# A cross-attention kernel's scores: from one f32 product to three f16 products, with another order of steps

## The reference

```python
# x: (64, 32, 256); ctx_1024: (64, 257, 128); H = 16 heads of D = 128
h = layernorm(x)
q = rmsnorm((h @ Wq).reshape(B, 32, 16, 128), gq)
k = rmsnorm((ctx @ Wk).reshape(B, 257, 16, 128), gk)
v = (ctx @ Wv).reshape(B, 257, 16, 128)
scores = einsum("bqhd,bkhd->bhqk", q, k) / sqrt(128)
x = x + (softmax(scores) @ v).reshape(B, 32, 2048) @ Wo
x = x + self_attention(layernorm(x))        # ternary weights, rope, causal, 32 tokens
x = x + moe(layernorm(x))                   # 8 experts, capacity 256, and a shared one
```

## Time and profile before

| | |
|---|---|
| runs, median (lowest to highest) | 1541.29 us (1538.57 to 1545.86) |
| profiled execution, its own time | 1538.1 us |
| its span | 1536.3 us |
| mean granted TensorE clock | 0.936 |
| TensorE busy | 1295.5 us, 84% |
| VectorE busy | 1005.7 us, 65% |
| ScalarE busy | 841.6 us, 55% |
| GpSimd busy | 538.5 us, 35% |

### The profile page before, as it was taken

One profiled execution on the slowest core, in us unless ns is written; L12 is line 12 of the kernel. 1 busy time (PEld: TensorE's weight loads), 2 busy tenths in 40 slices (PEclk: granted clock), 3 DMA queues, 4 the chain that ended last, 5 costly groups with the idle time before them and its releaser, 6 DMA issues.

```text
span 1536.3 us, 35628 instructions
## 1 busy us (share of the span) xinstructions
PE 1295.5 (84%) x10526; PEld 881.2 (57%) x10526; DVE 1005.7 (65%) x3748; ACT 841.6 (55%) x3560; POOL 538.5 (35%) x1337
## 2 busy tenths in 40 slices
PE   5768898989899898989898989888898989864881
PEld 2545666566666556565666565656565565643761
DVE  6846677677767677777777776777776767743112
ACT  5365566656475656666565666475656556631110
POOL 2044342524352534435243525342524325310003
PEclk9998999999999999999999999999999989985996
DMA  9000000000010101000001000000101000100544
GB/s 372 22 26 12 23 15 25 17 25 17 11 32 10 32 7 30 13 25 17 21 14 28 14 25 18 14 28 11 31 7 35 7 25 14 62 6 23 168 146 127
DMA packets 41191, 59.65 MB, mean 39 GB/s; under 512 B 5094, under 2 KB 35953, under 8 KB 40096
## 3 DMA queue, kind: packets, MB, share of 16 engines
q1 hardware_dynamic: 36880, 50.73, 10.3%
q0 software_dynamic: 2064, 6.14, 1.2%
q10 hardware_dynamic: 2176, 2.10, 0.4%
HBM read 48.62 MB, written 10.49 MB: 38 GB/s over the span
## 4 chain that ended last, share of the span: by engine, by line
PE 33%; issue 25%; POOL 16%; DVE 9%; ACT 5%; DMA 3%; POOLq 1%; SPq 0%; DVEq 0%; ACTq 0%
PE AB L594 21%; PE Eb L594 5%; POOL prob L1177 4%; PE Db L594 4%; ACT prob L1020 2%; DMA ctxn<-expert_rows 2%; POOL pjunk L1132 2%; PE C L719 1%; POOL cn_lo L1197 1%; DVE o_halves L1492 1%; POOL rstd L1152 1%; ACT rkb L1014 1%; POOL cl_rows L1212 1%; POOL c_lo L1138 1%; DVE kst L1312 1%
## 5 line engine op out<-in xcount | busy, mean ns | idle before, releaser
L950 ACT ACTIVATE AB<-AB 128x128 f32<-128x128 f32 (+1 forms) x1160 | 303.7, 262 | 185.4 <-PE AB L594 182.9
L1132 POOL TENSOR_TENSOR pjunk<-pjunk 128x1 f32<-128x1 f32 x288 | 56.3, 196 | 683.9 <-DVE sinv L1482 365.9
L594 PE MATMUL AB<-wk_hi,c_hi 128*128 128x512 f16 x512 | 199.7, 390 | 22.0 <-POOL c_lo L1138 8.8
L1312 DVE BATCH_NORM_STATS2 kst<-AB 128x6 f32<-128x256 f32 x512 | 181.3, 415 | 55.4 <-PE AB L594 50.9
L950 ACT ACTIVATION_READ_ACCUMULATOR AB<-AB 128x1 f32 (+1 forms) x1160 | 216.0, 186 | 0.0
L594 PE MATMUL AB<-wk_lo,c_hi 128*128 128x512 f16 x512 | 198.5, 388 | 0.0
L594 PE MATMUL AB<-wk_hi,c_lo 128*128 128x512 f16 x512 | 197.5, 386 | 0.0
L594 PE MATMUL AB<-ctxT,qpT 128*128 128x257 f32 x512 | 161.6, 472 | 35.5 <-DVE sc L1547 27.4
L1020 ACT ACTIVATE prob<-prob,nbias,rq 128x257 f32<-128x257 f32 x256 | 150.4, 590 | 7.9 <-DVE nbias L1477 7.9
L594 PEld LDWEIGHTS AB<-ctxT,qpT 128*128 128x128 f32 x512 | 115.2, 236 | 60.6 <-DVE sc L1547 29.1
L1177 POOL TENSOR_SCALAR prob<-prob,sinv 128x257 f32<-128x257 f32 x256 | 128.7, 503 | 20.2
(11 more groups left out here) (252 smaller groups left out, 2933.9 us busy)
## 6 DMA issues: line engine op xcount, KB each, us to landing
ctxT<-in_ctxT SPq DMA_DIRECT2D x64, 128.5 KB, 2.1
ctxn<-in_ctxn SPq DMA_DIRECT2D x64, 128.0 KB, 2.1
wq_hi<-in_w SPq DMA_DIRECT2D x4, 768.0 KB, 5.3
wq_lo<-in_w SPq DMA_DIRECT2D x4, 768.0 KB, 5.6
expert_rows<-base POOLq DMA_DIRECT2D x1, 2048.0 KB, 15.8
xin<-in_x SPq DMA_DIRECT2D x16, 128.0 KB, 2.2
prob<-in_wqT SPq DMA_DIRECT2D x1, 2048.0 KB, 19.2
xres<-in_x SPq DMA_DIRECT2D x16, 128.0 KB, 2.0
```

What stands on the lines that cost most here:

```text
L594: return pe.matmul(out, lhsT, rhs, start=start, stop=stop)
L950: ins = nc.scalar.activation(k, k, ACT.Square, accum_out=sums[0:m, h:h + 1])
L1132: own.mark(pool.tensor_tensor(pjunk[:, 0:1], pjunk[:, 1:2], pjunk[:, 1:2], ALU.mult))
L1312: ins = V.bn_stats(stats[:, 0, 2 * half + n], AB[0:m, 2 + half, 2 * D * n:2 * D * (n + 1)])
```

## The change

The projected queries are kept as two f16 halves instead of one f32 value. ScalarE's copy in QP now writes the high half and leaves the bank filled; VectorE has a new step QP, which subtracts the high half from the bank, writes the low half and gives the bank back. A score bank is now made by three f16 matmuls, high by high, high by low and low by high, from the halves `c_hi` and `c_lo` of the keys that GpSimd has made already. And all four lists of the loop are in another order; in the first fill only VectorE's new QP is put in.

```diff
@@ ORDER, the list of VectorE, before and after @@
-    "DVE": """K0 X K1 K2 dp3 XL K3 KN0 Q do3 RQ f K4 K5 qkv K6 s0 i0 sc s1 sm K7 KN1 ys yv i1 dp0 pr ln2 do0 dp1
-              s2 lg do1 i2 up pos s3 dn dp2 do2 i3""".split(),
+    "DVE": """K0 X K1 K2 XL dp3 K3 do3 KN0 Q RQ f K4 K5 K6 qkv QP s0 K7 KN1 i0 sc s1 sm dp0 ys yv s2 pr ln2 i1 s3
+              i2 do0 up lg dp1 dn pos i3 do1 dp2 do2""".split(),
...
-        qpT = sb("qpT", [P, NB, H * SQ])
+        qpT = sb("qpT", [P, 2, NB, H * SQ], F16)
...
+        qp_ready = Events(sem("qp_ready"), pro=BANKS, full=BANKS)
...
+        def query_part(e, n):
+            return qpT[:, e, :, 4 * SQ * n:4 * SQ * (n + 1)].rearrange("p b (h q) -> p h b q", q=SQ)
+
+        def by_query(n):
+            return AB[:, n].rearrange("p (h b q) -> p h b q", b=NB, q=SQ)
...
-                    mm(AB[:, g, 0:SKV], qpT[:, b, P * g:P * (g + 1)], ctxT[:, SKV * b:SKV * (b + 1)])\
-                        .then_inc(filled[s].sem, 1)
+                    q_hi, q_lo = (qpT[:, e, b, P * g:P * (g + 1)] for e in range(2))
+                    keys_hi, keys_lo = (c[:, SKV * b:SKV * (b + 1)] for c in (c_hi, c_lo))
+                    mm(AB[:, g, 0:SKV], q_hi, keys_hi, stop=False)
+                    mm(AB[:, g, 0:SKV], q_hi, keys_lo, start=False, stop=False)
+                    mm(AB[:, g, 0:SKV], q_lo, keys_hi, start=False).then_inc(filled[s].sem, 1)
...
-                    nc.scalar.copy(dst, src).then_inc(drained[s].sem, 1)
+                    nc.scalar.copy(query_part(0, n), by_query(n)).then_inc(qp_ready.sem, 1)
...
+            def step_QP(p):
+
+                for n, s in enumerate(BANKS):
+                    dve.wait_ge(qp_ready.sem, qp_ready.at(p, s))
+                    V.tensor_tensor(query_part(1, n), by_query(n), query_part(0, n), ALU.subtract).then_inc(drained[s].sem, 1)
```

More of the change, by code:

```diff
@@ L149 @@
 ORDER = {
[L150 to L153, removed]
-    "DVE": """K0 X K1 K2 dp3 XL K3 KN0 Q do3 RQ f K4 K5 qkv K6 s0 i0 sc s1 sm K7 KN1 ys yv i1 dp0 pr ln2 do0 dp1
-              s2 lg do1 i2 up pos s3 dn dp2 do2 i3""".split(),
-    "POOL": """h1 h0 c2 n3 h2 X c3 r0 cl ln1 c0 h3 r1 n0 c1 r2 y n1 ln2 r3 n2 scat""".split(),
+    "PE": """K0 pt3 K1 K2 X K3 o3 Q f K4 K5 xt1 K6 qkv rk1 rk0 QP qk s0 K7 sc s1 rk2 pt0 pv s2 st pr rk3 s3 o0
+              xt2 up lg pt1 dn pos o1 pt2 o2""".split(),
+    "ACT": """K0 tl3 K1 K2 X ph3 K3 oh3 Q K4 K5 xt1 K6 qkv rk1 rk0 QP qk K7 e0 sc rk2 ph0 tl0 pv e1 rk3 e2 xt2 oh0
+              up ph1 tl1 lg e3 oh1 ph2 tl2 oh2""".split(),
+    "DVE": """K0 X K1 K2 XL dp3 K3 do3 KN0 Q RQ f K4 K5 K6 qkv QP s0 K7 KN1 i0 sc s1 sm dp0 ys yv s2 pr ln2 i1 s3
+              i2 do0 up lg dp1 dn pos i3 do1 dp2 do2""".split(),
+    "POOL": """h0 n3 h1 X h2 c1 c3 c0 r1 ln1 h3 c2 r0 cl r2 n0 r3 y ln2 n1 n2 scat""".split(),
 }
@@ L164 @@
               K7 ph1 tl1 oh0 rk2 e2 rk3 oh1 e3 ph2 tl2 oh2""".split(),
-    "DVE": """low wk KL KNL K0 K1 X K2 XL wql K3 gg KN0 Q W0l wt0 W1l K4 RQ wt1 M01 wt K5 M23 tw s0 s1 i0 K6 dp0
+    "DVE": """low wk KL KNL K0 K1 X K2 XL wql K3 gg KN0 Q W0l wt0 W1l K4 QP RQ wt1 M01 wt K5 M23 tw s0 s1 i0 K6 dp0
               i1 K7 KN1 do0 dp1 s2 s3 i2 dp2 do1 i3 do2""".split(),
@@ L445, in build @@
         fin = [x[:, :].rearrange("p b n -> p (b n)").rearrange("p (a c) -> p a c", c=DIM) for x in
-               (qpT, rkx[:].rearrange("p a k n -> p (a k) n"))]
+               (qpT[:].rearrange("p e b n -> p e (b n)").bitcast(F32), rkx[:].rearrange("p a k n -> p (a k) n"))]
         fin = [f[:, 4 * k:4 * k + 4] for f in fin for k in range(2)]
@@ L956, in step_QP @@
                     act.wait_ge(filled[s].sem, filled[s].at(p, "QP"))
-                    dst = qpT[:, :, 4 * SQ * n:4 * SQ * (n + 1)].rearrange("p b (h q) -> p h b q", q=SQ)
-                    src = AB[:, n].rearrange("p (h b q) -> p h b q", b=NB, q=SQ)
-                    nc.scalar.copy(dst, src).then_inc(drained[s].sem, 1)
+                    nc.scalar.copy(query_part(0, n), by_query(n)).then_inc(qp_ready.sem, 1)
             def step_X(p):
@@ L1629, in step_dn @@
                 V.tensor_tensor(base[:], x2[:], Eb[:, 0:DIM], ALU.add).then_inc(drained["E"].sem, 1)
-            steps = dict(X=step_X, XL=step_XL, Q=lambda p: key_stats(p, "Q", P, qst), RQ=step_RQ,
+            steps = dict(X=step_X, XL=step_XL, Q=lambda p: key_stats(p, "Q", P, qst), RQ=step_RQ, QP=step_QP,
                          wql=step_wql, W0l=lambda p: step_Wl(p, 0), W1l=lambda p: step_Wl(p, 1), f=step_f, qkv=step_qkv, sc=step_sc, sm=step_sm, ys=step_ys, yv=step_yv,
```

## The result

The changed kernel took 1525.3 us, the median of 7 runs (1523.58 to 1530.19), beside 1541.3 us for the kernel before: a ratio of 0.991, 95% interval 0.988 to 0.994. One of the seven runs of the kernel before that were timed beside it, 1620.6 us, stands far above the other six (1534.5 to 1545.9) and is not in the ratio.

The account below looks back on a forecast made before the run. It took the loop as half bound by TensorE, half by a chain through VectorE. 1538.1 less 15 for the loop plus 2 for the ends gave 1525, in the median about 1528; it said 1527, range 1501 to 1552.

Parts of the forecast that it names:

- 1.0 a tile: Loop: a tile of 81.1 us against 82.0 to 82.2, taken as 15 us over fifteen tiles.
- The score products: TensorE's score steps: 1.73 to 1.30 us each at full clock, 1.7 us a tile, up to 2.6.
- Nothing hides it: VectorE's four subtractions between qkv and s0: 0.62 us each, 2.5 a tile, covered only by what TensorE does meanwhile.
- Rival (3): Subtraction on VectorE at its upper bound, 1.03 us each: 1.6 us more a tile, 1551 us; chance 0.10.
- The walk: One tile followed in the new order: K0 to QP 37.7 us, pv at 59.4, then 21.7 to the next K0.
- "+1" for the first fill: First fill: four subtractions (2.5 us) behind VectorE's K4, TensorE's score steps 1.7 shorter; 1 us longer.
- "+1" for the last tile: Last tile: up and dn come ahead of pos, so the experts' scatter is about 1 us later.
- s2, if it stays at half clock, 0.8: Between pv and the next K0: s2's shorter score products take 0.8 us off if the half clock remains.
- Rival (2): Half clock lasting until pr and o0: about 1.7 us a tile, 25 above the forecast, 1552 us; chance 0.09.
- the rule of the Trainium skill: TensorE's clock: throttled by default, released by activity; shorter score products and longer waits around sc speak against the change.

Follow-up runs that it names:

- the kernel with the fill's edit alone: Changed kernel with VectorE's QP moved behind RQ in the first fill only; 1521.6 us, 0.988 of the kernel before.
- the kernel of two products with extra matmuls: Changed kernel without the low-by-high score product, plus 13 unread matmuls a tile behind sc and rk2; 1524.3 us, 0.991 of the kernel before.

## Why the prediction was right, and where its terms were wrong

The number, 1527 against 1525.3, is as near as it is by luck: its errors offset each other. The loop gives 23.9 us in 14 periods where 1.0 a tile was taken (14), and the last tile 1.9 where nothing was left (1.0 less 1); against that the fill costs 7.0 where 1 was, and the experts' part 5.0 where none was.

**The score products** were right: 1.32 us a step at full clock, 0.33 a bank, 2.55 at half. Between the f32 and the f16 kernel in the new order they give 1.6 us a tile of the 1.7 that they hold.

**"Nothing hides it"** was wrong as the new order has it. The size of the subtraction was right, 0.62 us. But "VectorE's chain gets 2.5 us longer while TensorE's work gets 1.7 us shorter" sets against each other two things that lie side by side. QP and qk end on TensorE at the same time whether VectorE subtracts meanwhile or not: s0 starts 43.3 us behind K0 in the f32 kernel in the new order and 43.4 in the changed one. The sentence holds in the old order, where K6 waits 2.04 us and a tile gains nothing. The walk itself had both paths, K7 on TensorE and the statistics at 49.0 (48.4 measured), so the sum did not suffer from it. Rival (3) was not far off in its price for all that: with 0.2 us of cover left at s0's last bank, 0.41 more for each of four would have put about 1.4 us on the path (an estimate from these two numbers).

**The walk**, K0 to QP 37.7, to pv 21.7, to K0 21.7, measured 37.1, 21.9 and 21.6 in the tile shown. The 0.6 is in the first stretch, in waits that came out 0.9 shorter together, with 0.3 of small gaps against them that were not followed: pt3 was to wait 0.5 for n3 and waits under 0.2 (K0's twelve products end at 774.93 + 2.6 = 777.5, pt3 starts at 777.69), so n3 does not hold it up, rk0 0.4 and waits 0.24, K5 1.71 and waits 1.23. From QP to pv the waits came out singly too: 1.07, 2.16, 0.53 us before sc, before s1 and before pt0 (0.5 to 1.5 there over the 14 tiles), where 1.0, 2.4 and 0.9 were said. The other 0.1 of the 0.7 by which the gain of a tile was short is the base: "82.0 to 82.2" is the steady tile, as the median is, and the loop's mean before is 82.3 by its one period of 85.6.

**"+1" for the first fill** is the term that was most mis-sized. It counted four subtractions of 0.62 as work. They stand in line behind QP's banks, so the step lasts from the first to the last bank, 5.2 us with what it waits, and RQ and the weight work behind it come as much later. A row that tells of it stood in the trace before: ScalarE's copy of a bank waits 0.86 us for TensorE.

**"+1" for the last tile** was wrong in its sum. With the loop's last turn in it, which the sum counted as its fifteenth tile, that part should have come out even, and took 1.9 us less. The turn itself lasts the same in both traces (80.5 and 80.6 us from K0 to the end of o2). Behind it, pr to the last scatter takes 17.3 us where it took 15.7, later as the term says (16.5 in the kernel with the fill's edit alone), but o2 to pr takes 39.4 instead of 43.0, which the term left out: pt3 there waits 1.3 us for GpSimd instead of 5.1, since i3 and with it n3 come earlier in the new lists (n3 itself waited 4.3 us for i3 before, and after not at all). Giving the router its old order back is worth 0.3 to 0.4.

**The clock.** "s2, if it stays at half clock, 0.8" was left open; it got its full clock back, and with the order alone. From pv to pr it takes 4.6 us before and 3.5 in the new order with either product, but hardly for the clock: in three tiles of the kernel before s2 has its full clock already, and these take 4.35. The rest fits KN1, which stood on VectorE between sm and ys (754.94 to 758.09) and is now ahead of sc. Rival (2), the half clock that lasts into pr, costs what was said, about 1.7 us a tile (medians 81.6 against 79.8 in the kernel of two products with extra matmuls), but it did not come in this kernel: pr takes 1.97 us in all 14 tiles, and in the one tile where the half clock lasts over s2 up to pr it took 81.8 us. Leaving out a third of the score products brought it into 12 of 14. With the extra matmuls it came in 7. So the trace agrees with the rule of the Trainium skill, "TensorE: Matmul & The Clock Gate", section "What's actually happening", that activity releases the throttle; that the rule speaks against shorter score products was true one step further on.

## What to carry to other kernels

A step that drains several banks as another engine fills them costs its queue the time from the first bank to the last, not its own busy time: put ahead of it what others wait for. What covers an added operation is read from the neighbours in the new list, with the last instruction that needs it; here four subtractions fitted with at most 0.2 us to spare, and the same four in the old list made TensorE wait 2.04 us. A mean over tiles can mix kinds: before a cost is put down to a wait, compare tiles with the same clock. A removed product can lower the clock of what comes next; look at the granted clock of each stretch, not at busy time, before a saving between weak stretches is counted.

## What the runs showed that was not expected

Leaving out a third of the score products made the loop 1.3 us a tile slower, at a mean clock of 0.915 instead of 0.937, and putting 13 useless matmuls into the waits took 1.2 us off again, at 0.957. The eight f32 matmuls of pr take 1.97 us at full clock and 3.49 where it fell, and these 1.5 us are nearly the whole distance between the two kinds of tile (81.39 against 79.77). The same eight matmuls, at 1.97 or 3.76 us, split the tiles of the f16 kernel in the old order (82.1 to 82.2 against 84.4 to 85.9), where a wait of 2.04 us stands in every tile and by itself made none of them longer than before.
